# Gated conv pair, last round: the Relu of block 104 goes to GpSimd, the last gate no longer stands behind it on ScalarE

## What is computed

```
yp = conv3x3(x[:, :16], w[:, :16])
yr = conv3x3(x[:, 16:], w[:, 16:])
y  = bn(yp + sigmoid(2 * (yp - theta)) * yr)
```

## Time and profile before

| | |
|---|---|
| median of 3 runs | 434.79 us (434.56, 434.79, 436.45) |
| profiled execution, its own time | 434.86 us |
| its span, first to last instruction | 433.0 us |
| outside the span | 434.86 - 433.0 = 1.86 us |
| granted TensorE clock, mean | 0.995 |
| DVE, ACT, POOL busy | 57%, 46%, 7% |

### The profile page before, as it was taken

How to read it: one execution, slowest core, us unless ns; L and a number is a source line. 1 busy time by engine, 2 the same in 40 slices (tenths; PEclk the granted TensorE clock), 3 DMA queues, 4 the chain that set the end, 5 groups by cost and what they waited for, 6 DMA issues and landing times.

```text
span 433.0 us, 17317 instructions
## 1 busy us (share of the span) xinstructions
PE 425.9 (98%) x7817; PEld 423.0 (98%) x7817; DVE 246.6 (57%) x420; ACT 198.8 (46%) x337; POOL 30.2 (7%) x83
## 2 busy tenths in 40 slices
PE   9999999999999999999999999999999999999994
PEld 7999999999999999999999999999999999999993
DVE  6767644753764663574375385366357367436535
ACT  5765444534544553453453453354345355434322
POOL 6041000000000100000000000011000000000001
PEclk9999999999999999999999999999999999999998
DMA  8435116241515110420624161161623322012044
GB/s 170 83 78 99 27 27 124 50 98 30 122 28 101 25 28 3 100 51 2 125 58 81 37 122 30 27 122 25 122 49 61 67 49 45 8 27 49 8 93 94
DMA packets 119802, 27.57 MB, mean 64 GB/s; under 512 B 119408, under 2 KB 119664, under 8 KB 119728
## 3 DMA queue, kind: packets, MB, share of 16 engines
q1 hardware_dynamic: 117296, 25.99, 29.4%
q10 hardware_dynamic: 2112, 0.46, 0.5%
q0 software_dynamic: 320, 0.00, 0.0%
HBM read 13.60 MB, written 12.85 MB: 61 GB/s over the span
## 4 chain that ended last, share of the span: by engine, by line
PE 97%; DVE 1%; issue 0%; ACT 0%; POOL 0%; DVEq 0%; POOLq 0%
PE acc L554 96%; PE acc L500 1%; DVE mix L858 0%; DVE rows_out L906 0%; PE acc L494 0%; PE acc L580 0%; ACT mix L697 0%; DVE rows_out L948 0%; DVE rows_out L903 0%; POOL h_lo L437 0%; ACT rows_out L719 0%; DVEq L857 0%; POOLq L960 0%
## 5 line engine op out<-in xcount | busy, mean ns | idle before, releaser
L554 PE MATMUL acc<-x_lo,w_hi 32*128 32x456 f32 (+1 forms) x1392 | 248.4, 358 | 0.0
L554 PE MATMUL acc<-x_hi,w_lo 32*128 32x456 f32 (+1 forms) x1392 | 248.2, 358 | 0.0
L554 PE MATMUL acc<-x_hi,w_hi 32*128 32x456 f32 (+1 forms) x1392 | 247.7, 358 | 0.0
L554 PE MATMUL acc<-h_hi,w_lo 32*128 32x512 f32 x1152 | 241.4, 390 | 0.0
L554 PE MATMUL acc<-h_lo,w_hi 32*128 32x512 f32 x1152 | 241.0, 390 | 0.0
L554 PE MATMUL acc<-h_hi,w_hi 32*128 32x512 f32 x1152 | 240.7, 389 | 0.0
L554 PEld LDWEIGHTS acc<-x_hi,w_hi 32*128 32x128 f32 x1392 | 208.5, 183 | 0.4
L554 PEld LDWEIGHTS acc<-x_hi,w_lo 32*128 32x128 f32 x1392 | 208.6, 183 | 0.2
L554 PEld LDWEIGHTS acc<-x_lo,w_hi 32*128 32x128 f32 x1392 | 208.5, 183 | 0.0
L554 PEld LDWEIGHTS acc<-h_hi,w_hi 32*128 32x128 f32 x1152 | 181.3, 183 | 0.1
L554 PEld LDWEIGHTS acc<-h_lo,w_hi 32*128 32x128 f32 x1152 | 181.3, 184 | 0.1
(11 more groups left out here) (85 smaller groups left out, 157.3 us busy)
## 6 DMA issues: line engine op xcount, KB each, us to landing
out_dram<-rows_out SPq DMA_DIRECT2D x95, 126.0 KB, 2.6
x<-in_x_dram SPq DMA_DIRECT2D x28, 392.0 KB, 5.3
early<-in_x_dram SPq DMA_DIRECT2D x4, 112.0 KB, 4.0
out_dram<-rows_out SPq DMA_DIRECT2D x3, 112.0 KB, 2.8
x<-in_x_dram SPq DMA_DIRECT2D x3, 98.0 KB, 3.8
x<-in_x_dram SPq DMA_DIRECT2D x1, 294.0 KB, 4.2
x<-in_x_dram SPq DMA_DIRECT2D x1, 280.0 KB, 4.9
x<-in_x_dram SPq DMA_DIRECT2D x1, 196.0 KB, 4.1
```

Of the source, the lines that this page charges most:

```text
L554: return pe.matmul(sums(bank, blk), w[g * ROWS:(g + 1) * ROWS, tap], moving(blk, part, c, dx, g), start=(u == 0 and (alone or g == bank_gr ...
```

## The change

ScalarE's `finish` returns at once for block 104 (m = 46 = `ON_POOL`). GpSimd does that block's shift and Relu in place as one `tensor_scalar` (add, then max with 0), placed in its program ahead of its add for block 107, and signals on a semaphore of its own, `pool_ready`. SP's store of m = 46 waits for that semaphore. As ScalarE's counter `out_ready` now skips one block, `by_scalar(m)` gives the count that the others wait for: m + 1 below m = 46, m above.

```diff
+    ON_POOL = len(second) - ROUND
+
+    def by_scalar(m):
+        return m + (m < ON_POOL)
...
+        pool_ready = sem("pool_ready")
...
                 if m == len(second) - 1:
                     sp.wait_ge(last_ready, 1)
+                elif m == ON_POOL:
+                    sp.wait_ge(pool_ready, 1)
                 else:
-                    sp.wait_ge(out_ready, m + 1)
+                    sp.wait_ge(out_ready, by_scalar(m))
...
+            m = ON_POOL
+            pool.wait_ge(summed_ready, place[second[m]] + 1)
+            nc.gpsimd.tensor_scalar(out_of(m), out_of(m), shift[:, 1:2], 0.0, ALU.add, ALU.max).then_inc(pool_ready, 1)
 
             m = len(second) - 1
             pool.wait_ge(za_ready, NA + 1)
...
             def finish(b):
                 kind, n = order[b]
+                if kind != "a" and second_of[kind, n] == ON_POOL:
+                    return
...
                 if m >= BY_TWO:
-                    act.wait_ge(out_ready, m + 1)
+                    act.wait_ge(out_ready, by_scalar(m))
                     store_half(nc.scalar, m, 1)
```

## The result

The changed kernel is slower: its time over that of the kernel before is 1.0026, with a 95% interval from 1.0014 to 1.0039, over 21 and 21 runs (one more of each, at 525 and 857 us, is left out). That is 1.1 us, where 0.1 us of gain was forecast. It lies within the 0.5% that the forecast called "same", and outside its range, which ended at 435.5: the median is 436.85 us, beside 436.44 for the kernel before in the same session.

A forecast was written before the change was run, and what follows sets the result against it. TensorE bounds the kernel, and queued store transfers set its end; data ending at 432.02 instead of 432.12 gains 0.10 us, so 434.86 - 0.10 = 434.76, forecast as 434.75, range 434.2 to 435.5.

The forecast's parts named there:

- ScalarE's gate: Block 107's gate on ScalarE begins 0.52 us earlier, at about 424.91; block 105's Relu 0.39 earlier, at 426.16.
- VectorE and `z_last`: In the tail no VectorE step moves; `z_last` and GpSimd's add come earlier, but that stays hidden.
- Rival C: Block 107's gate did hold VectorE, so its last four steps come up to 0.52 us earlier: 434.5 us; chance 0.04.
- GpSimd's Relu, X: Length of GpSimd's new Relu of block 104: 1.03 us, from the copies, bounded by 0.47 and 1.27.
- The rule of the Trainium skill: One-input GpSimd bodies run at 1.03 cycles per element: about 0.43 us plus overhead for block 104's Relu; not in the sum.
- 3.0 cycles with the overhead: Price per element of GpSimd's two-input add of block 107, from 1133 / 448 = 2.5 ns.
- The stores, and the sum: Tail stores: data ends at the later of 431.85 and 430.99 plus the GpSimd Relu's length, against 432.12 before.
- A: GpSimd's Relu of block 104 is as dear as its add, 1.13 to 2.05 us; 2.05 gives 435.8; chance 0.24.
- GpSimd's Relu is above 2 us: One of the signs, at block 104's Relu on GpSimd, by which the forecast would count itself wrong.
- B: Slower by over 0.5% (2.17 us) through GpSimd's Relu, at 3.30 us or more, as a costly first execution; chance 0.02.
- D: Block 107's gate and block 105's Relu stay where they are, its input coming only at about 425.4: 434.86 to 435.0; chance 0.06.

The follow-up runs named there:

- experiment 1: The changed kernel with block 104's shift and Relu left out: 434.38 us against 434.75 for the kernel before, ratio 1.000.
- Experiment 4: The kernel before with 21 extra GpSimd instructions of several forms on scratch, where GpSimd was idle: 435.0 us in its one run, against 434.75.
- experiment 2: The changed kernel with GpSimd's shift and Relu of block 104 done twice: 437.38 us against 434.75 for the kernel before, ratio 1.006.

## Why the prediction was wrong

- **ScalarE's gate**: right. 424.90 for 424.91, block 105's Relu at 426.16 as worked out, block 106's unmoved, and a worth of 0.27 us of data by itself (0.30 in experiment 1).
- **VectorE and `z_last`**: right. Nothing moved. ("Each instruction begins a few hundredths before the recorded end of the one in front" misreads: half of them begin 0.03 or 0.04 behind it. Nothing hangs on it.) Rival C, the chain of waits taken at its word, falls: the gate came 0.53 us earlier and the product of block 106 did not.
- **GpSimd's Relu, X**: this is the step that failed. I took 1.03 us from the copies and held 1.27, the two-input add, for a bound from above "since it has one input". It measured 1.97. Both choices took GpSimd's price to be that of moving elements in and out. Experiment 4 shows that it goes with the form of the instruction: copy 0.60, two-input add 1.28, `tensor_scalar` with one operation 1.48 and with two 1.90. The difference between 504 and 252 columns (1.97 - 1.13) gives 3.3 ns for each element and 0.3 us fixed. I extrapolated the copies badly as well, 1.03 for a true 0.60, from two means that mixed quick and slow ones: one by one, the copies in the trace of the kernel before take 0.22 or 0.23 us for 57 elements and 0.28 for 114, or else 0.50 to 0.68, and the quick ones alone give 0.28 + 390 / 57 x 0.05 = 0.62.
- **The rule of the Trainium skill** (GPSIMD Engine Reference, section 3.1), 1.03 cycles for each element with one input and few operations: the trace does not agree for this instruction. 3.3 ns are an estimated 4.0 cycles at the 1.2 GHz that the page gives. It would have led further off than the copies. The prediction's "3.0 cycles with the overhead" for the add was loose too: 1.28 us for 504 elements and 1.13 for 448 are 2.5 ns for each in both, which leaves no overhead to take off.
- **The stores, and the sum**: right in kind and nearly in size. With the true X it gives 432.96 - 432.12 = +0.84 us of data, and the trace has +0.90. From 1.13 to 1.97 the last data moves 0.76 us for 0.84 us of X. Beyond that the rule overstates, since ScalarE's two stores don't stand behind SP's. What stays open is the rest of the time: +1.12 where the data has +0.90. From the last data to the end of the span 0.97 us pass in the changed kernel and 0.84 in the one before; in the nine other runs it is 0.84 to 0.96, with spans given to 0.1. No run here says more, and the remaining 0.1 is about what the groups scatter.
- **The rivals**: A comes nearest, and it had 0.24. GpSimd's Relu was dear and lies inside the 1.13 to 2.05 given there, and of its grounds the second operation was real (0.42 us); but its heading, "as dear as its add", fell short as well, by 0.7 us. Its own example, 2.05, gave 435.8, and the lower group's 435.79 meets that partly by luck: with X = 1.97 the sum gives 434.86 + 0.84 = 435.70, from a base 0.19 above the lower group's, and a loss of 0.84 where 1.12 was measured. The range stopped at 435.5 because it trusted 1.27. The sign "GpSimd's Relu is above 2 us" was set too high for the same reason: 1.97 doesn't trip it, and the forecast was wrong all the same. B falls, since 1.1 us is half of its 2.17, and no first use was dear: the two Relus of experiment 2 took 1.97 each. D falls with the gate at 424.90.

## What to carry to other kernels

A price for an engine's operation that the trace doesn't show is not bounded from above by a row of another form, however much more that one seems to do: the two-input add took 1.28 us, and `tensor_scalar`, with one input and as few operations, 1.48. Where no row has the form, there is no upper bound to state, and the form can be measured first, on scratch, in a stretch where the engine is idle. Before moving a step to a slower engine to free 0.5 us of another, ask what its output feeds: here the tail was a row of transfers, and its end was fixed by when the first of them could begin and by every pause after, so the first store was the last one that should have been made late. Reordering the stores gave nothing back here, because the next block's were ready no earlier than the late first one.

## What was not expected of the hardware

- On GpSimd `tensor_scalar` in fp32 is dearer than a two-input add of the same size: 1.48 to 1.97 us against 1.28 for 128x504. VectorE did the same shift and Relu in 0.48.
- VectorE felt GpSimd's probes in places. In experiment 4 the sum that reads two tiles of SBUF took 1.02 to 1.08 us, not 0.74, in the three cases where it began within 0.2 us behind a `tensor_scalar`'s start on GpSimd, and 0.74 where it began 0.9 into one. VectorE's timeline, for the first of the three and for the last case (GpSimd's instructions began at 408.60 and 411.81):

```profile
408.69 1.06 DVE L930 SCALAR_TENSOR_TENSOR rows_out<-mix,inv,rows_out 128x504 f32<-128x504 f32 x1
...
412.67 0.74 DVE L930 SCALAR_TENSOR_TENSOR rows_out<-mix,inv,rows_out 128x504 f32<-128x504 f32 x1
```

  In the changed kernel the VectorE steps beside the new Relu read one of their inputs from PSUM, and kept their 0.67 and 0.74.
